# Expert slots of a mixture layer: the far slots' chain cut into parts on VectorE, the owners' comparisons as one product, the place marks on GpSimd

## What is computed

```python
logits = xf @ gate_w.T                       # 1024 x 32
w, idx = jax.lax.top_k(logits, 2)
w = jax.nn.softmax(w, axis=-1)
combine = zeros((T, 32)).at[arange(T)[:, None], idx].add(w)
def body(acc, params):
    W, b, c = params
    return (acc + c[:, None] * (xf @ W.T + b), None)
out, _ = jax.lax.scan(body, zeros_like(xf), (expert_w, expert_b, combine.T))
x = x + tanh(g_ffn[1]) * out
```

## Time and profile before

| | us |
|---|---|
| median of three runs | 917.7 |
| lowest, highest run | 916.02, 917.77 |
| span of the profiled execution | 912.7 |
| PE busy in the span | 840.6 (92%) |
| DVE, POOL, ACT busy | 656.2, 427.1, 397.0 |

### The profile page before, as it was taken

How to read it: one execution, slowest core, us unless ns; L and a number is a source line. 1 busy time by engine, 2 the same in 40 slices (tenths; PEclk the granted TensorE clock), 3 DMA queues, 4 the chain that set the end, 5 groups by cost and what they waited for, 6 DMA issues and landing times. The chain is left out here.

```text
span 912.7 us, 13118 instructions
## 1 busy us (share of the span) xinstructions
PE 840.6 (92%) x4337; PEld 702.5 (77%) x4337; DVE 656.2 (72%) x1300; ACT 397.0 (43%) x1009; POOL 427.1 (47%) x386
## 2 busy tenths in 40 slices
PE   5878999999999999999999999977989999989990
PEld 4766888888888888888888888866878687777870
DVE  3776888766778876778876688774473557999975
ACT  4634334333424424325333433434124446878970
POOL 5488447535436634635733643512020048876730
PEclk9999999999999999999999999998999969999995
DMA  8302101101101100200300120006100556999817
GB/s 333 155 1 93 70 1 59 59 1 47 70 1 46 69 0 0 77 39 0 115 0 0 46 92 1 1 1 239 55 1 12 205 211 223 356 333 342 324 38 277
DMA packets 23641, 91.13 MB, mean 100 GB/s; under 512 B 6576, under 2 KB 7088, under 8 KB 15776
## 3 DMA queue, kind: packets, MB, share of 16 engines
q1 hardware_dynamic: 17440, 81.00, 24.1%
q0 software_dynamic: 6144, 9.46, 2.9%
HBM read 86.23 MB, written 14.68 MB: 111 GB/s over the span
## 5 line engine op out<-in xcount | busy, mean ns | idle before, releaser
L361 POOL TENSOR_TENSOR qT<-straight,turned 128x512 f32<-128x512 f32 x64 | 82.5, 1290 | 147.5 <-DVE turned L572 147.5
L458 ACT ACTIVATE probs<-bank,negmax 128x128 f32<-128x128 f32 x256 | 90.5, 365 | 130.3 <-DVE negmax L583 130.2
L572 DVE TENSOR_TENSOR turned<-bank,sinT 64x512 f32<-64x512 f32 x160 | 110.2, 688 | 2.2
L134 PE MATMUL bank<-wo_hi,oT_hi 128*128 128x512 f32 x256 | 101.3, 396 | 8.0 <-DVE oT_lo L596 6.2
L134 PE MATMUL bank<-xT_hi,wq_hi 128*128 128x512 f32 x256 | 105.7, 413 | 1.1 <-POOL wq_lo L340 1.1
L135 PE MATMUL bank<-xT_lo,wq_hi 128*128 128x512 f32 x256 | 101.5, 397 | 0.0
L136 PE MATMUL bank<-xT_hi,wq_lo 128*128 128x512 f32 x256 | 101.3, 396 | 0.0
L135 PE MATMUL bank<-wo_lo,oT_hi 128*128 128x512 f32 x256 | 100.6, 393 | 0.0
L136 PE MATMUL bank<-wo_hi,oT_lo 128*128 128x512 f32 x256 | 100.6, 393 | 0.0
L465 ACT ACTIVATE pT_hi<-bank 128x512 fp32r<-128x512 f32 x64 | 38.3, 598 | 133.1 <-PE bank L738 133.1
L570 DVE TENSOR_TENSOR straight<-bank,cosT 128x512 f32<-128x512 f32 x80 | 55.3, 691 | 48.2 <-PE bank L136 43.7
(11 more groups left out here) (228 smaller groups left out, 2101.3 us busy)
## 6 DMA issues: line engine op xcount, KB each, us to landing
ring<-in_ew SPq DMA_DIRECT2D x28, 1024.0 KB, 8.5
raw_big<-in_wq SPq DMA_DIRECT2D x8, 1024.0 KB, 4.8
raw_big<-in_wo SPq DMA_DIRECT2D x8, 1024.0 KB, 4.8
early_w<-in_ew SPq DMA_DIRECT2D x8, 1024.0 KB, 8.1
ring<-picked SPq DMA_DIRECT2D x8, 512.0 KB, 7.3
raw_k<-in_wk SPq DMA_DIRECT2D x8, 256.0 KB, 5.0
ctx_raw<-in_ctxT SPq DMA_DIRECT2D x4, 512.0 KB, 5.9
raw_v<-in_wv SPq DMA_DIRECT2D x8, 256.0 KB, 4.8
```

Source lines behind the costliest of these rows:

```text
L134: nc.tensor.matmul(out_, hi, r_hi, start=start, stop=False)
L361: nc.gpsimd.tensor_tensor(dst, straight[:, k, :], turned[:, k, :], ALU.add).then_inc(rope_sum, 1)
L458: ex = nc.scalar.activation(probs[:, u % 2, h, :], bank_scores[u % 2][:, h * S:(h + 1) * S], ACT.Exp, bias=negmax[:, u % UNITS, h:h + 1], ...
L572: last = nc.vector.tensor_tensor(turned[dst, k, :], bank[src, :], sinT[src, tok], ALU.mult)
```

## The change

The six instructions of `far_slots()` are spread, one behind each of the slots 12 to 17. `owners()` moves from slot 16 to slot 11; its 16 comparisons become one tensor_tensor of 128x512, put behind slot 10. `far_places` leaves DVE: POOL makes the 16 marks instead, each a tensor_scalar of 128x128, one behind each scatter of the slots 2 to 17. `far_rows()` goes from ahead of `multiply(14)` to ahead of `multiply(20)` and now waits for all 16 marks; `write_rows` goes from slot 15 to slot 21.

```diff
@@ POOL
+                def far_place(pair):
+                    nc.gpsimd.tensor_scalar(at_far[:, pair, :], numbers[:, :], rest[:, pair:pair + 1], None, ALU.is_equal).then_inc(far_at, 1)
...
                     give(k)
+                    if k == 2:
+                        pool.wait_ge(m_step, 9)
+                    if 2 <= k < 18:
+                        far_place(k - 2)
@@ DVE
-                def far_slots():
+                def far_slot_of_pairs(part):
...
-                def far_places(half):
-                    pairs = slice(half * NB, half * NB + NB)
-                    nc.vector.tensor_tensor(at_far[:, pairs, :], numbers[:, :].unsqueeze(1).broadcast_to([P, NB, P]),
-                                            rest[:, pairs].unsqueeze(2).broadcast_to([P, NB, P]), ALU.is_equal).then_inc(far_at, 1)
+                def owners_passed():
                     ready()
+                    step(nc.vector.tensor_tensor(passed[:, :, :], summed_to.unsqueeze(1).broadcast_to([P, 16, NX]),
+                                                 numbers[:, 0:16].unsqueeze(2).broadcast_to([P, 16, NX]), ALU.is_le))
                 def owners():
-                    for j in range(16):
-                        last = nc.vector.tensor_scalar(passed[:, j, :], summed_to, float(j), None, ALU.is_le)
-                    step(last)
...
                     if k == 10:
-                        far_slots()
-                    if k in (11, 12):
-                        far_places(k - 11)
-                    if k == 15:
+                        owners_passed()
+                    if k == 11:
+                        owners()
+                    if 12 <= k < 18:
+                        far_slot_of_pairs(k - 12)
+                    if k == 21:
                         dve.wait_ge(far_laid, 1)
                         write_rows(slice(NX, SLOTS), psum[3][:, 0:EXTRA], 1)
-                    if k == 16:
-                        owners()
@@ PE
-                    pe.wait_ge(far_at, 2)
+                    pe.wait_ge(far_at, NB * TOP)
...
-                    if k == 14:
+                    if k == 20:
                         far_rows()
```

More of the change, by code:

```diff
@@ L1419, in far_starts @@
                     step(nc.vector.tensor_tensor(first_far[:, :], summed_to, last_full_i[:, :], ALU.subtract))
-                def far_slots():
+                def far_slot_of_pairs(part):
                     pairs = [P, NB * TOP, NX]
                     ready()
-                    step(nc.vector.tensor_tensor(far_weighted[:, :, :], onehot[:, :, :, :].bitcast(F32).rearrange("p t k e -> p (t k) e"),
-                                                 first_far[:, :].unsqueeze(1).broadcast_to(pairs), ALU.mult))
-                    ready()
[L1428 to L1439, removed]
@@ L1441, in far_places @@
-                def far_places(half):
-                    pairs = slice(half * NB, half * NB + NB)
-                    nc.vector.tensor_tensor(at_far[:, pairs, :], numbers[:, :].unsqueeze(1).broadcast_to([P, NB, P]),
-                                            rest[:, pairs].unsqueeze(2).broadcast_to([P, NB, P]), ALU.is_equal).then_inc(far_at, 1)
+                    if part == 0:
+                        step(nc.vector.tensor_tensor(far_weighted[:, :, :], onehot[:, :, :, :].bitcast(F32).rearrange("p t k e -> p (t k) e"),
+                                                     first_far[:, :].unsqueeze(1).broadcast_to(pairs), ALU.mult))
+                    elif part == 1:
+                        step(nc.vector.tensor_reduce(far_slot[:, :], far_weighted[:, :, :], AX.X, ALU.add))
+                    elif part == 2:
+                        step(nc.vector.tensor_tensor(far_slot[:, :], far_slot[:, :], full[:, :], ALU.add))
+                    elif part == 3:
+                        step(nc.vector.scalar_tensor_tensor(far_slot[:, :], full[:, :], 0.0, far_slot[:, :], ALU.is_gt, ALU.mult))
+                    elif part == 4:
+                        step(nc.vector.tensor_tensor(in_far[:, :, :], numbers[:, 1:17].unsqueeze(1).broadcast_to([P, NB * TOP, 16]),
+                                                     far_slot[:, :].unsqueeze(2).broadcast_to([P, NB * TOP, 16]), ALU.is_equal))
+                    else:
+                        nc.vector.tensor_tensor(far_code[:, :, :], in_far[:, :, :],
+                                                pair_codes[:, :, :].rearrange("p t k -> p (t k)").unsqueeze(2).broadcast_to([P, NB * TOP, 16]),
+                                                ALU.mult).then_inc(far_built, 1)
```

## The result

The changed kernel takes 932.9 us (median of five runs, 930.4 to 937.3) against 917.4 before: ratio 1.0172, interval 1.0151 to 1.0194, 15.5 us slower. The forecast was 924.6, 6.9 us slower, with an upper end of 930, which the result passes. The sign was right; the loss is more than twice the forecast one.

A forecast was written before the change was run, and what follows sets the result against it. In slots 4 to 11 PE, POOL and ACT were taken as level; with marks, POOL's 4.15 us turns put multiply(20) 6.9 us later, so 917.7 + 6.9 = 924.6 us. The range was 913.5 to 930.

The forecast's parts named there:

- POOL's turn decides: At far_rows, PE waits for all 16 POOL marks, so multiply(20) starts at 842.7 against 835.84, 6.9 us later.
- 4.15 us a turn: POOL's gather, scatter and mark per slot: the turn taken, between 3.9 and 4.5, puts mark 15's end at 840.9.
- the sum: At POOL's last mark: mark 0's end at 778.6 plus 15 turns of 4.15 us gives 840.9.
- The walk by rows: POOL's first turns followed against DVE's subtractions in the earlier trace: 4.1, 4.1, then 5.2 us, 4.5 over three.
- if starts fell at random: POOL's turn with half of three starts held by half a subtraction, some 0.8 us together: 3.9 us.
- slips in ahead: POOL's gather behind a mark starts before DVE's next subtraction and is not held; twice in the three turns followed.
- Far matmuls 1.8 us, then slots at 3.27: PE behind the last mark: far matmuls take 1.8 us, then slots run at 3.27 us with no further loss.
- DVE's 3.8 us "if nothing else is late": Spreading the DVE work cuts PE's waits: PE alone would reach multiply(20) at 832.1 against 835.84, 3.8 us gained.
- A mark holds DVE up by nothing: DVE beside POOL's marks: the sum has no delay term; marks holding DVE stand only in the 929.8 us rival.
- Every start held: Rival on POOL: gather, scatter and mark all hit, 4.5 us or more a turn, 929.8 us; chance 0.16.
- Hidden: Rival on POOL: it keeps up, turn under 3.45 us, only DVE's gain is left, 913.9 us; chance 0.19.

The follow-up runs named there:

- the second trace of the kernel before: The kernel before, unchanged, run once more for another trace: span 916.0 us, time 917.8 us.
- the one-input product: The changed kernel with DVE's weight subtraction replaced by a product of the weights with zero: 916.0 us, ratio 0.9985 to the kernel before.
- marks on GpSimd and six lanes: The changed kernel with six result lanes instead of four and far_rows ahead of multiply(23): 925.8 us, ratio 1.0084 to the kernel before.
- the filled wait: The changed kernel with 22 matmuls on data of no use ahead of PE's wait for the last mark: 933.8 us, ratio 1.0189 to the kernel before.

## Why the forecast was right in sign and too small

**POOL's turn decides: right.** The last mark sets `multiply(20)`, PE's longest wait is there, marks take 0.62 to 1.80 us, POOL has no idle time but its steps as long as marks are left, and behind slot 20 PE runs at 3.26. The marks alone on POOL cost as much as the whole change; off POOL nothing is lost.

**4.15 us a turn: the term that was mis-sized.** It is 4.50. Over 15 turns that is 5.3 us, and mark 0 ends 0.7 later than in the sum (779.34 against 778.6): mark 15 ends at 846.86 instead of 840.9, 6.0 us. The failed step is the choice of 4.15. The walk by rows had come to 4.5 over three turns; what pulled the term down was the 3.9 of "if starts fell at random", with half of three starts held, 0.8 us together. In the trace 29 of 45 starts are held, 0.63 us each, 1.23 us a turn. The rest is a free turn of 3.27 us, not 3.12, most of it because a gather behind a mark needs 1.11 us when nothing holds it, not 1.02. The starts do not fall at random: a held mark ends 0.47 to 0.49 us after the subtraction that held it, where only that one did, and so the next start is set by DVE too. Where a mark meets a slot's first subtraction, the second follows 0.5 us on and takes the gather; four of the eight held gathers come about so.

That the walk came to 4.5 was partly luck. It used DVE's times of the trace before, in which its three marks met a slot's second subtraction, behind which DVE often waits. So the gather "slips in ahead" in two turns of three; in the trace it does so in seven of 15, and the other eight gathers take 1.65 us or more. In return the walk had every mark held and two scatters of three, the trace 12 marks and nine scatters of 15.

**Far matmuls 1.8 us, then slots at 3.27: wrong.** They took 3.41 at a granted clock of 0.50, and slot 20 took 4.89, most of it at the same clock (matmuls of 0.63 us, then of 0.40): 1.6 + 1.7 = 3.3 us that no term of the sum held. For these two traces the sum closes: 6.9 + 6.0 + 3.3 = 16.2, the lateness of `multiply(21)`. Both are of short executions: against the second trace of the kernel before, `multiply(21)` is 12.3 us late (842.96 there). The other four executions of the change take 2.2 to 6.9 us more than the profiled one, at a mean granted clock of 0.953 to 0.958 over the run instead of 0.964; no trace shows where. That these matmuls were slow at the lower clock is in the rows. Why the clock fell was not settled: with PE busy through most of the wait it still fell, behind the far matmuls.

**DVE's 3.8 us "if nothing else is late": not measured as it stands, its condition not met.** No run has the DVE part with the marks hidden elsewhere. With the marks on DVE as two comparisons, which the prediction's own terms put at 2.1 us, the part is worth some 3 us with six lanes (914.4) and nothing with four (917.4). What is late next is the scatter that ACT's copy waits for. The waits on it stood in the earlier trace rows, and the prediction used them only to show that POOL is full. In the forecast itself this changed nothing, since POOL was later still.

**A mark holds DVE up by nothing: right within 0.1.** Three subtractions start while a mark runs, at 783.58, 787.62 and 838.86, and take 1.23, 1.32 and 1.23 us instead of 1.22.

**The rivals.** "Every start held", 4.5 us a turn and 929.8, was the nearest: its turn is the measured one, though not every start is held. It, too, lacked the clock. "Hidden" needed 3.45; even with DVE's operation at 0.69 instead of 1.22 the turn was 3.77.

## What to carry to other kernels

Before moving work to GpSimd, count each of its starts in the turn, not only the new one: where DVE runs 1.2 us operations a short step apart, an instruction held by one releases the next straight into the other. A wait that is added to TensorE costs more than its length when the granted clock falls behind it, here 3.3 us behind a wait of 6.2, so give the clock its own term. And a part that frees one engine may show its gain only when the next limit goes too: here the same edit was worth nothing with four result lanes and 3 us with six, while the lanes alone were worth nothing.

## What the runs showed of the hardware that was not expected

A one-input tensor_scalar of 128x1024 on DVE (0.69 us) holds a GpSimd transfer as a two-input subtraction (1.22 us) does; a gather behind a mark ended 0.96 us after the subtraction of 793.13 in the change and 0.97 us after the one-input product of 776.68. The operation with an input in PSUM did not hold the mark that began in it, which took 0.63 us.

GpSimd took longer for the same work beside a fuller DVE. A gather, a scatter and a mark took 3.77 us a turn beside the short product (DVE busy for 0.66 of the stretch), 4.50 in the change (0.79), and 4.97 with marks on GpSimd and six lanes (0.82). The share alone does not give the turn: in the trace of the filled wait it was 4.68 at 0.79.

The same mark of 128x128 takes 0.60 to 0.63 us on GpSimd when nothing holds it, 0.28 at best on DVE.
